# Hybrid block on one core: the scan's input term moved to PSUM, state sums by four halves, first normalisation on ScalarE, and an order of its own for the last batch

## What is computed

```python
x = x + ssm(layernorm(x))          # dt = softplus(...)*0.099+0.001, per token and channel
    # h[d,n] = exp(dt[d]*A[d,n]) * h[d,n] + inp[n],  inp[n] = sum_d dt[d]*A[d,n]*u[d]*B[n]
    # y[d] = sum_n h[d,n]*C[n] + Dp[d]*u[d]
x = x + ffn(layernorm(x))          # fp4-rounded linears: silu(gate)*up, 256 -> 704 -> 256
x = x + linear_attention(layernorm(x))   # 16 heads of 16, running kv state
x = x + ffn(layernorm(x))          # the same weights again
```

## Time and profile before

| | us |
|---|---|
| three runs: median (lowest to highest) | 3253.51 (3250.42 to 3253.9) |
| the profiled execution, its own time | 3258.51 |
| its span, first to last instruction | 3256.8 |
| mean granted TensorE clock | 0.884 of 2.4 GHz |

### The profile page before, as it was taken

The page is one execution under the profiler, slowest core; times in us unless marked ns, Lnnn a source line. Parts: engine busy times, 40 slices in busy tenths (PEclk is TensorE's granted clock), DMA queues, the critical chain, the costliest instruction groups (busy, mean ns, idle before and its releaser), DMA issues.

```text
span 3256.8 us, 44290 instructions
## 1 busy us (share of the span) xinstructions
PE 2547.0 (78%) x12844; PEld 1449.3 (45%) x12908; DVE 2482.7 (76%) x4197; ACT 1884.0 (58%) x3613; POOL 1127.5 (35%) x1601
## 2 busy tenths in 40 slices
PE   3438788797879888797978879697887979787875
PEld 1104445353535445363544535354453535445553
DVE  6468787978778797878879797788868788776642
ACT  3356657574755657475655748466574746644331
POOL 2003243433434343333334333343333334333331
PEclk8569799898989899898989989899988989888896
DMA  2344433434343333434333343334334343331000
GB/s 61 68 72 60 53 50 46 62 42 66 38 60 49 51 53 46 63 40 64 44 50 51 46 66 39 60 44 54 52 42 66 39 65 43 53 43 26 4 4 7
DMA packets 95654, 157.96 MB, mean 49 GB/s; under 512 B 10722, under 2 KB 29358, under 8 KB 95406
## 3 DMA queue, kind: packets, MB, share of 16 engines
q1 hardware_dynamic: 95406, 154.96, 34.3%
HBM read 12.33 MB, written 8.39 MB: 6 GB/s over the span
## 4 chain that ended last, share of the span: by engine, by line
PE 32%; DVE 21%; ACT 18%; issue 10%; DMA 8%; SPq 6%; POOL 5%; DVEq 0%; ACTq 0%; POOLq 0%
DMA scan_bufs<-dt 7%; PE bank L938 6%; PE bank L921 6%; SPq L480 6%; DVE scan_bufs L1210 4%; ACT p_xT L647 4%; DVE rounding L1077 3%; PE bank L978 2%; PE acc_y L886 2%; PE bank L959 2%; PE bank L918 2%; POOL f_h L565 2%; ACT scan_bufs L637 2%; ACT masked_scores L688 2%; DVE f_h_max L1104 2%
## 5 line engine op out<-in xcount | busy, mean ns | idle before, releaser
L1210 DVE TENSOR_TENSOR_SCAN scan_bufs<-scan_bufs,inp 128x512 f32<-128x512 f32 x512 | 714.0, 1394 | 66.5 <-ACT scan_bufs L639 56.7
L637 ACT ACTIVATE scan_bufs<-scan_bufs,a_rows 128x512 f32<-128x512 f32 x512 | 366.4, 716 | 345.8 <-DMA scan_bufs<-dt 343.9
L921 PE MATMUL bank<-w_gu,f_xqT 128*128 128x512 f32 x1024 | 509.3, 643 | 30.2 <-ACT f_xqT L688 28.5
L886 PE MATMUL acc_y<-scan_bufs,sel_y 128*32 128x512 f32 x1024 | 308.8, 685 | 225.7 <-DVE scan_bufs L1220 225.2
L938 PE MATMUL bank<-w_dn,f_hqT 128*128 128x256 f32 (+1 forms) x1536 | 425.8, 424 | 34.1 <-issue 24.8
L565 POOL TENSOR_TENSOR f_h<-f_h,f_h_inv 128x704 f32<-128x704 f32 x128 | 222.9, 1742 | 484.4 <-DVE f_h_inv L1108 484.4
L938 PEld LDWEIGHTS bank<-w_dn,f_hqT 128*128 128x128 f32 (+1 forms) x1536 | 301.4, 209 | 172.8 <-issue 131.5
L1220 DVE TENSOR_TENSOR scan_bufs<-scan_bufs,c_bank 128x512 f32<-128x512 f32 x512 | 338.2, 661 | 8.1 <-DVE x L1238 1.7
L583 POOL TENSOR_SCALAR_AFFINE_SELECT masked_scores<-masked_scores 128x512 f32<-128x512 f32 x256 | 190.2, 767 | 436.1 <-ACT masked_scores L688 436.1
L639 ACT ACTIVATE scan_bufs<-scan_bufs 128x512 f32<-128x512 f32 x512 | 322.6, 630 | 16.2
L565 POOL TENSOR_TENSOR f_h<-f_h,f_h_scale 128x704 f32<-128x704 f32 x128 | 195.7, 1529 | 388.8 <-DVE f_h L1079 388.8
(11 more groups left out here) (192 smaller groups left out, 4710.4 us busy)
## 6 DMA issues: line engine op xcount, KB each, us to landing
scan_bufs<-dt SPq DMA_DIRECT2D x512, 256.0 KB
xp<-L_attn_a_x SPq DMA_DIRECT2D x16, 512.0 KB, 7.6
out<-x SPq DMA_DIRECT2D x64, 128.0 KB, 1.7
w_attn<-L_attn_b_W_attn SPq DMA_DIRECT2D x1, 768.0 KB
scan_bufs<-L_ffn_w_gate SPq DMA_DIRECT2D x1, 704.0 KB
scan_bufs<-L_ffn_w_up SPq DMA_DIRECT2D x1, 704.0 KB
masked_scores<-L_ffn_w_down SPq DMA_DIRECT2D x1, 704.0 KB
w_in<-L_attn_a_w_in SPq DMA_DIRECT2D x1, 256.0 KB, 2.8
```

What stands on the lines that cost most here:

```text
L637: nc.scalar.activation(half, half, ACT.Exp, scale=a_rows[:, c, at:at + 1]).then_inc(root_ready, 1)
L886: last = nc.tensor.matmul(acc_y[32 * j:32 * j + 32, :], sel_y[:, q, :], bar[n % SLOTS][:, h, :], start=(q == 0), stop=(q == 3), tile_posit ...
L921: last = nc.tensor.matmul(to[:, :], f.xqT[:, k, :], w_gu[:, k, g, lo:hi], start=(k == 0), stop=(k == DH - 1))
L1210: nc.vector.tensor_tensor_scan(half, half, inp[par][:, :], 0.0, ALU.mult, ALU.add)\
```

## The change

- `inp` becomes a PSUM bank of its own, with one copy; `B` goes to a new SBUF tile `b_rep`, and DVE multiplies it with bank G into `inp`. The scan (L1210) reads its second input from PSUM. Five banks are left to be given out.
- PE sums four halves in one visit (`sum_states`, eight visits a batch in place of 16), after the last of the four has been read. Both slots are reported as summed one after the other within the visit. The spreads have a part of their own (D), still one for each slot.
- P's normalisation moves from DVE to ACT, as four ACTIVATEs with scale and bias; POOL gets two more operations of four elements a partition for the bias.
- After the loop the four bodies are replaced by one list, `TAIL`, sorted by absolute beat, with banks given out anew. In it R2 of the last batch begins at beat 88 with a gap of 3, in place of 95.7 with a gap of 7.
- Most beats are changed by fractions to about one beat. Of the tables only a few lines are shown.

```diff
-PARTS_AT = {"P": (0, 0, 1), "M": (32, 1, 32), "G": (32, 2, 16), "S": (48.75, 16, 2), "Y": (65, 1, 2), "R1": (66, 3, 4), "R2": (95.7, 7, 4)}
+PARTS_AT = {"P": (0, 0, 1), "M": (32, 1, 32), "D": (32, 2, 16), "G": (32, 4, 8), "S": (48.75, 16, 2), "Y": (65, 1, 2), "R1": (66, 3, 4), "R2": (95.7, 7, 4)}
+
+LAST_AT = {"R1": (66, 3), "R2": (88, 3)}
...
-        ("P", "load"): 2.8, ("G", "spread"): -1.75, ("R2", "down"): 12.8,
+        ("P", "load"): 1.35, ("D", "spread"): -3.05, ("R2", "down"): 14.8,
...
-        ("P", "B"): 16.5, ("P", "C"): 32.25, ("P", "dt0"): 20.5, ("P", "dt1"): 23.7, ("P", "G"): 29.6,
-        ("G", "sum"): 2.85, ("Y", "turn"): 0.2, ("R1", "turn_x"): 4.8, ("R1", "up0"): 6.3, ("R1", "up1"): 7.3,
...
+        ("P", "B"): 16.6, ("P", "C"): 32.4, ("P", "dt0"): 20.5, ("P", "dt1"): 23.5, ("P", "G"): 30.6,
+        ("G", "sum"): 4.85, ("Y", "turn"): 0.15, ("R1", "turn_x"): 5.3, ("R1", "up0"): 6.5, ("R1", "up1"): 7.3,
...
-        ("P", "stats"): 4.2, ("P", "norm"): 5.05, ("P", "dt0"): 23.3, ("P", "dt1"): 26.05, ("P", "inp"): 30.8,
-        ("M", "scan"): -0.03, ("M", "read"): 0.6, ("S", "skip"): -0.1, ("Y", "finish"): 0.01, ("R1", "stats"): 0.3,
...
+        ("P", "stats"): 5.1, ("P", "dt0"): 23.6, ("P", "dt1"): 25.85, ("P", "inp"): 31.95, ("M", "scan"): 0.3,
+        ("M", "read"): 0.7, ("S", "skip"): -0.4, ("Y", "finish"): 0.01, ("R1", "stats"): 0.45, ("R1", "norm"): 1.8,
...
+def beat_of(engine, part, step, t, b):
+
+
+    at = start_of(engine, part, step, t)
+    if b == NB - 1 and part in LAST_AT:
+        first, gap = LAST_AT[part]
+        at += first - PARTS_AT[part][0] + t * (gap - PARTS_AT[part][1])
+    return round(BEATS * b + at, 6)
...
+def tail_of(engine):
+
+
+    steps = [(beat_of(engine, part, step, t, b), b, t, part, step) for b in range(NB) for part, step in TIMES[engine]
+             for t in range(PARTS_AT[part][2]) if BEATS * b + start_of(engine, part, step, t) >= BEATS * LOOP_TO]
+    return [(b, part, t, step) for _, b, t, part, step in sorted(steps, key=lambda z: z[:3])]
...
+        free = [0.0] * count
+        for i in range(LOOP_TO):
+            for k, part, t, use, at, until in uses:
                 if 0 <= i - k < NB:
                     j = given[part, t, use]
-                    seen[j] += 1
-                    self.nth[part, t, use, i - k] = (j, seen[j])
-
-    def bank_of(self, part, t, use):
-
-        return self.nth[part, t, use, 0][0]
+                    free[j] = max(free[j], BEATS * i + until)
+                    next_use(part, t, use, i - k, j)
+        for b, part, t, step in TAIL["pe"]:
+            for use, engine, drained in made_by(part, t, step):
+                j = min(range(count), key=lambda n: (free[n], n))
+                free[j] = max(beat_of("pe", part, step, t, b), beat_of(engine, part, drained, t, b))
+                next_use(part, t, use, b, j)
...
-        inp = [sb(f"inp{i}", [P, T]) for i in range(2)]
+        b_rep = sb("b_rep", [P, T])
...
-        acc_y, c_rep = bank("acc_y"), bank("c_bank")
-        banks = [bank(f"bank{j}") for j in range(6)]
+        acc_y, c_rep, inp = bank("acc_y"), bank("c_bank"), bank("inp_bank")
+        banks = [bank(f"bank{j}") for j in range(5)]
...
-            for i in range(LOOP_TO, BODIES):
-                run(i, i)
-
-        def batches(i, par, steps):
-
-            for k, part, t, step in steps:
+            run(LOOP_TO, 0)
+
+        def batches(i, par, engine):
+
+            if isinstance(i, int) and i == LOOP_TO:
+                for b, part, t, step in TAIL[engine]:
+                    yield b, b % 2, part, t, step
+                return
+            for k, part, t, step in ORDER[engine]:
...
+                    pool.tensor_tensor(p_below[:, :], p_mv[:, :, 0], minus_one[:, :].broadcast_to([P, TILES]), ALU.mult)
                     pool.tensor_tensor(p_rstd[:, :], p_var[:, :], minus_half[:, :], ALU.pow).then_inc(p_rstd_ready, 1)
+                    pool.wait_ge(p_rstd_ready, upto(b, 1, 0))
+                    pool.tensor_tensor(p_below[:, :], p_below[:, :], p_rstd[:, :], ALU.mult).then_inc(p_below_ready, 1)
...
+                if step == "norm":
+                    act.wait_ge(x_loaded, upto(b, 1, 0, 16))
+                    act.wait_ge(p_below_ready, upto(b, 1, 0))
+                    if not first(b):
+                        wait_drained(act, "P", b - 1, 0, "G")
+                    for c in range(TILES):
+                        last = nc.scalar.activation(p_xn[:, c, :], xp[par][:, c, :], ACT.Identity,
+                                                    bias=p_below[:, c:c + 1], scale=p_rstd[:, c:c + 1])
+                    last.then_inc(p_normed, 1)
...
-                    evac(step, inp[par][:, :])
+                    if not first(b):
+                        wait_drained(act, "P", b - 1, 0, "G")
+                    evac(step, b_rep[:, :])
...
-            def sum_state(b, n):
-
-                pe.wait_ge(read_out, upto(b, HALVES, DH * n + DH - 1))
-                if n == NS // DH:
+            def sum_states(b, t):
+
+                pe.wait_ge(read_out, upto(b, HALVES // 4, t, 4))
+                if t == 4:
                     pe.wait_ge(skip_ready, upto(b, DH, 0))
-                elif n == 0 and not first(b):
+                elif t == 0 and not first(b):
                     pe.wait_ge(skip_ready, upto(b - 1, DH, 1))
-                for h in range(DH):
-                    j, q = divmod(rows_of(DH * n + h)[1], 4)
+                for m in range(4 * t, 4 * t + 4):
+                    n, h = divmod(m, DH)
+                    j, q = divmod(rows_of(m)[1], 4)
                     last = nc.tensor.matmul(acc_y[32 * j:32 * j + 32, :], sel_y[:, q, :], bar[n % SLOTS][:, h, :],
                                             start=(q == 0), stop=(q == 3), tile_position=(0, 32 * j),
                                             skip_group_check=True)
-                last.then_inc(summed, 1)
+                    if h == DH - 1:
+                        last.then_inc(summed, 1)
...
-                elif step == "norm":
-                    dve.wait_ge(p_rstd_ready, upto(b, 1, 0))
-                    for c in range(TILES):
-                        last = nc.vector.tensor_scalar(p_xn[:, c, :], xp[par][:, c, :], p_mv[:, c, 0:1],
-                                                       p_rstd[:, c:c + 1], ALU.subtract, ALU.mult)
-                    last.then_inc(p_normed, 1)
...
-                    nc.vector.tensor_tensor(inp[par][:, :], inp[par][:, :], src[:, :], ALU.mult).then_inc(done, 1)
+                    if not first(b):
+                        dve.wait_ge(scans_done, upto(b - 1, HALVES, HALVES - 1))
+                    nc.vector.tensor_tensor(inp[:, :], b_rep[:, :], src[:, :], ALU.mult).then_inc(done, 1)
...
-                nc.vector.tensor_tensor_scan(half, half, inp[par][:, :], 0.0, ALU.mult, ALU.add)\
+                nc.vector.tensor_tensor_scan(half, half, inp[:, :], 0.0, ALU.mult, ALU.add)\
...
-                        if first(b) and step in ("norm", "dt0", "dt1"):
-                            round_weights(("norm", "dt0", "dt1").index(step))
+                        if first(b) and step in ("stats", "dt0", "dt1"):
+                            round_weights(("stats", "dt0", "dt1").index(step))
```

More of the change, by code:

```diff
@@ L492, in run @@
             def run(i, par):
[L493 removed]
+                for b, q, part, t, step in batches(i, par, "sp"):
                     if step == "load":
@@ L771, in run @@
             def run(i, par):
-                for b, q, part, t, step in batches(i, par, ORDER["act"]):
+                for b, q, part, t, step in batches(i, par, "act"):
                     if part == "M":
@@ L1034, in run @@
             def run(i, par):
-                for b, q, part, t, step in batches(i, par, ORDER["pe"]):
+                for b, q, part, t, step in batches(i, par, "pe"):
                     if step == "C":
```

40 lines of the change are left out of this document (23 added, 17 removed), and 41 rows, old and new, of the table TIMES.

## The result

| | before | after |
|---|---|---|
| median of 7 runs each (lowest to highest), us | 3253.51 (3246.88 to 3255.12) | 3239.58 (3230.83 to 3243.59) |
| ratio, 95% interval | 1 | 0.9956 (0.9942 to 0.9970) |
| span of the profiled execution | 3256.8 | 3229.1 |
| mean granted TensorE clock | 0.884 | 0.853 |

The change gives 14 us where 112 were forecast. It is faster, by 0.4% and clear of the interval, but the time lies above the whole range.

A forecast was written before the change was run, and what follows sets the result against it. No engine alone bounds: spreading DMAs, then PE with DVE, then PE lead. 5.5 us a batch over 13 batches (72) plus 41 at the end, from 3258.5, gives 3145.5, less 5.0 for the median: 3141 us; range 3065 to 3220.

The forecast's parts named there:

- one bank less: Shared PSUM banks: each drained at least 0.3 beats (1.8 us) before PE rewrites it; costed at nothing.
- later release of the slots: Slots freed in pairs after four-half sums: first spread has 7 us to spare, DMA-led pace stays; costed at nothing.
- The forecast's own sign of being wrong: Batch period of 187 us or more with PE's and DVE's busy time both down would show the forecast wrong.
- The scans: DVE scan with PSUM input escapes POOL's exclusion: 5.6 us a batch off DVE, 45% on the path, 2.5 us.
- The fixed cost of a PSUM source: Rival, chance 0.05: PSUM input slows each DVE scan by up to 60 ns, 25 us in all, giving 3166 us.
- Sums by four: PE state sums: eight visits of 1.2 us save 7.2 us of PE a batch, 2.5 us counted on the path.
- The second rival: Late slots take the gain back: net 1 us a batch and the end's 41 left, 3200 us, chance 0.15.
- The normalisation: First normalisation moved from DVE to ACT: 0.5 us a batch gained, between 1.6 and -1.
- The end: Last batch's second FFN starts earlier: 109 us in place of 150, 41 less, bounded by 61 and 20.
- The reading of the bound: Batch read by stretches: spreading DMAs set the first's pace, PE and DVE above 90% next, PE leads the last half.
- PE leads: Last 93 us of the batch: PE busy for 80.6 us, DVE 69.0, ACT 69.4, so PE was taken to lead.

The follow-up runs named there:

- before_psum_c_in_sbuf: Kernel before with the scan's input in PSUM and C copied by ACT to SBUF, so six shared banks, last bodies' banks given out anew: 3218.7 us, ratio 0.9900.
- after_old_end: Changed kernel with R2 of the last batch back at its old beats (gap of 7), all else as changed: 3263.0 us, ratio 1.0046 to the kernel before.
- after_c_in_sbuf: Changed kernel with C copied by ACT to SBUF, giving six shared banks while the scan's input stays in PSUM: 3312.9 us, ratio 1.0165 to the kernel before.

## Why the prediction was wrong

**Two steps failed, both costed at nothing: "one bank less" and "later release of the slots".** The first read the distance between ACT's copy and PE's next use from the tables' beats, at least 0.3 of a beat. But beats set only an order, and the engines run apart: ACT was some 5 us behind PE where it counted. Measured alone the bank costs 92 us, or about 40 once the scans are unblocked; either is more than the 32 us that the forecast took from the scans. So the part with the PSUM input, forecast at -32 us, measured +8 alone. The second step is larger by the same reckoning: the sums by four, forecast at -32 with the late release at nothing, measured +28 alone. The forecast's own sign of being wrong, a period of 187 us or more with both engines' busy time down, is what came.

**The scans**: the mechanism was right, and so was the term for DVE's busy time. The mean fell to 1213 ns against a median of 1218 forecast, 93 us of DVE. The 2.5 us a batch on the path is 2.6 by the periods of before and before_psum_c_in_sbuf, each good to about 1; where five banks made everything later, it was (194.5 - 188.3) = 6.2. The rule of the Trainium skill, page "SBUF — State Buffer", section "Who interferes with whom", was borne out both ways: no scan waits any more, and a read that moves to two SBUF inputs takes POOL's time again. The fixed cost of a PSUM source that the Trainium skill states (page "VectorE: DVE Perf Modes", section "The TRN2 errata — SBUF-src ops pay a fixed extra latency per instruction") did not show: 1159/1219 ns against 1158/1218.

**Sums by four**: the visit was forecast at 1.2 us and takes 1.06 at full clock, and PE has 105 us less to do. The 2.5 us a batch on the path was wrong in the old order (the period did not fall: 188.0 and 187.5) and so was **the late release at nothing**: its cover, 7 us of margin, does not exist where the spreads lead, and 21 us went in the first 577. That the release and not the moved beat of the spreads costs these 21 is read from the waits; the two were not changed apart. The second rival had this mechanism and the right place, and with 3200 came nearest; it lacked the bank. The view that would have told is the wait of ACT for spreads over the whole run, 343.9 us in 137 waits: at each of these the spread has no time to spare before its decay.

**The wait that the sum adds** was not priced for what is queued behind it. The longest waits for the fourth read, up to 21.7 us where it was 12.4, fall in the first 211 us. But from 900 us on PE stands once a batch, at its start, for 8.1 to 9.1 us, ten times in all, where before has no such wait over 8 us after its first 231 us. In the first 50 us of the batch from 1893 the granted clock is 0.76 where the earlier trace rows had 0.83. That the idle time lowers the clock was not tested apart.

**The normalisation** (6.5 us forecast, 14 and 11 measured, the 14 with the new banks of the last bodies in it) came with the right sign. **The end** came about as worked out: 41 forecast, 45 between the traces of the two kernels. Of the 45, R2's new beats give 28 by after_old_end; in the old order they give 44. The last four residual additions are 14.3 us apart in place of 24.4.

**The reading of the bound.** "PE leads" for the last 93 us hid that ACT is busy for 69.4 us of it and sets when banks are drained. PE, DVE and ACT are busy for 87, 74 and 75% of that stretch and tied to each other by banks and slots. That a saving on two of them is lost where the same change takes a bank and delays the slots is my reading of the runs; no run shows it by itself.

**What stays open.** In the old order the parts roughly add up: about -2 us, with the banks of the last bodies counted once by the estimate, against +10 measured for all four, and the new beats take 24 more, which gives the change's -14. But single parts undone in the changed order cost more than the same parts give in the old one, the PSUM input 68 us and the sums by four 77, both with the other sign. The old and the new beats were each laid for one set of parts, so a single swap prices the part and its misfit together; the 0.55 of a beat in after_c_in_sbuf is such a misfit. What a sixth bank is worth in the changed order, with beats that suit it, was not measured, and neither were the new banks of the last bodies by themselves.

## What to carry to other kernels

A buffer taken from a shared pool has a price in the trace, not in the schedule: look up for each use when the last reader really ran, and try the loss alone before counting a gain beside it. Where transfers lead, anything that frees their target later is paid in full at once. In an order written by hand, measure a part with and without it in both orders, and take together only what helped alone; here that is worth 112 us where the whole change gave 14. And look at what else the kernels of an experiment share: here all of one side had the banks of the last bodies given out anew, about 12 us that first seemed to belong to each part.

## What the runs showed of the hardware that was not expected

- At a jump back in a loop PE stands for 5.88 us in one kernel and DVE for 11.59 in another. Writing out the bodies, with four such jumps, gains 22 us in the second kernel and up to 48 of 3250 in the first.
- A scan with a PSUM input takes no longer than one with two SBUF inputs that POOL leaves alone, and it gives POOL more than DVE: with this part alone POOL is busy for 163 us less (964.4) and DVE for 114 (2368.6). In the changed kernel POOL's FFN multiplications go from 1742 and 1529 ns to 1390.
- The sum in four column tiles takes 1.06 us for eight records where half as many took 1.05.
